# The low part of a turned block, subtracted from the PSUM bank itself instead of from an ACT copy

## The reference

```
h      = layernorm(x)                        # 2048 tokens x 256
gates, experts = top2(h @ router)            # two of eight experts for each token
y[t]   = sum over the two: gate * (act(h[t] @ W1[e] + b1[e]) @ W2[e] + b2[e])
x      = x + tanh(g) * (y + shared experts)
```

## Time and profile before

| | |
|---|---|
| median of 3 runs | 1986.92 us (1980.81 to 1989.0) |
| span of the profiled execution | 2007.2 us |
| PE busy | 1773.6 us (88%) |
| DVE busy | 1262.0 us (63%) |
| ACT busy | 975.4 us (49%) |
| POOL busy | 528.7 us (26%) |

### The profile page before, as it was taken

How to read it: one execution, slowest core, us unless ns; L and a number is a source line. 1 busy time by engine, 2 the same in 40 slices (tenths; PEclk the granted TensorE clock), 3 DMA queues, 4 the chain that set the end, 5 groups by cost and what they waited for, 6 DMA issues and landing times. The chain is left out here.

```text
span 2007.2 us, 32563 instructions
## 1 busy us (share of the span) xinstructions
PE 1773.6 (88%) x11808; PEld 1447.6 (72%) x11808; DVE 1262.0 (63%) x2310; ACT 975.4 (49%) x1739; POOL 528.7 (26%) x492
## 2 busy tenths in 40 slices
PE   6998899967799996699999969998899789798895
PEld 4667799922577775699999558886577566688884
DVE  6886488546245553588887566765434688656643
ACT  4652476413687671377776234443433255317730
POOL 2220343254333341222220630002000144213333
PEclk9998799988799996699999979999699899899997
DMA  3003377420100000567775220000000100026742
GB/s 109 17 17 126 121 255 248 132 61 0 49 1 12 6 12 25 203 225 229 246 238 169 81 102 1 1 1 1 22 1 1 57 12 12 30 79 208 235 127 81
DMA packets 97139, 178.32 MB, mean 89 GB/s; under 512 B 25184, under 2 KB 61946, under 8 KB 95914
## 3 DMA queue, kind: packets, MB, share of 16 engines
q1 hardware_dynamic: 85496, 146.00, 22.0%
q0 software_dynamic: 11232, 30.69, 5.2%
q10 hardware_dynamic: 288, 0.00, 0.0%
HBM read 149.38 MB, written 27.26 MB: 88 GB/s over the span
## 5 line engine op out<-in xcount | busy, mean ns | idle before, releaser
L1667 POOL DMA_INDIRECT f_block_rows_home<-normed_x,f_token_of_sb x138 | 168.3, 1220 | 451.4 <-PE psum L1713 324.5
L1693 PE MATMUL psum<-f_block_h_sb,f_w1h_home 128*128 128x256 f32 x736 | 211.4, 287 | 30.2 <-issue 10.7
L1693 PE MATMUL psum<-f_block_l_sb,f_w1h_home 128*128 128x256 f32 x736 | 206.8, 281 | 0.0
L1693 PE MATMUL psum<-f_block_h_sb,f_w1l_home 128*128 128x256 f32 x736 | 206.7, 281 | 0.0
L2316 PE MATMUL psum<-a_xT_home,context_w 128*128 128x256 f32 x704 | 182.2, 405 | 13.6 <-PEq L122 9.7
L1703 PE MATMUL psum<-f_w2h_home,f_hidden_h_home 128*128 128x256 f32 x644 | 187.4, 291 | 2.0 <-DVE f_hidden_l_home L1887 1.0
L1703 PE MATMUL psum<-f_w2h_home,f_hidden_l_home 128*128 128x256 f32 x644 | 181.7, 282 | 0.0
L1703 PE MATMUL psum<-f_w2l_home,f_hidden_h_home 128*128 128x256 f32 x644 | 181.7, 282 | 0.0
L1693 PEld LDWEIGHTS psum<-f_block_h_sb,f_w1h_home 128*128 128x128 f32 x736 | 140.8, 191 | 38.5 <-issue 28.6
L2316 PEld LDWEIGHTS psum<-a_xT_home,context_w 128*128 128x128 f32 x704 | 132.6, 198 | 45.3 <-issue 20.0
L2481 ACT ACTIVATE a_probsT_sb<-psum 77x1024 f32<-77x1024 f32 (+1 forms) x128 | 130.7, 1021 | 69.0 <-PE psum L2368 66.5
(11 more groups left out here) (314 smaller groups left out, 3986.6 us busy)
## 6 DMA issues: line engine op xcount, KB each, us to landing
f_w_sb<-in_f_w SPq DMA_DIRECT2D x161, 512.0 KB
sorted_y<-f_result_sb SPq DMA_DIRECT2D x69, 256.0 KB
normed_x<-f_xn_all SPq DMA_DIRECT2D x24, 256.0 KB, 2.1
f_b_row_sb<-in_f_b SPq DMA_DIRECT2D x46, 128.0 KB
f_w_sb<-in_f_w SPq DMA_DIRECT2D x23, 256.0 KB
f_block_rows_home<-normed_x,f_token_of_sb POOLq DMA_INDIRECT x138
residual<-in_x SPq DMA_DIRECT2D x8, 256.0 KB, 6.2
context_w<-in_a_wk SPq DMA_DIRECT2D x2, 1024.0 KB, 5.0
```

The source lines that it names most:

```text
L1667: nc.gpsimd.indirect_dma_start(block_rows[b % 2][:, h, :], None, xs, bass.IndirectOffsetOnAxis(ap=column, axis=0)).then_inc(sems[f"rows_in ...
L1693: last = nc.tensor.matmul(hid_ps(q)[:, m, :], w, rhs, start=(j == 0), stop=(j == len(parts) - 1))
```

## The change

ACT's plain copy of the turned bank and its two buffers `block_T` are dropped. DVE's subtract reads the bank itself as its first operand, and `block_h` as before as its second. Since DVE is now the last to read the bank, the turn that writes into it next waits for `block_low` in place of `turned_out`, and so does the wait at the layer's end before the banks pass to other work.

```diff
--- before.py
+++ after.py
@@ -1509,7 +1509,6 @@
     home = lambda k: [env["homes"][name, f"{k}{q}"] for q in range(2)]
     hidden_h, hidden_l, block_rows = home("hidden_h"), home("hidden_l"), home("block_rows")
     w1h, w1l, w2h, w2l = home("w1h"), home("w1l"), home("w2h"), home("w2l")
-    block_T = [sb(f"block_T{s}", [P, DC, BLOCK]) for s in range(2)]
     block_h = [sb(f"block_h{s}", [P, DC, BLOCK], F32R) for s in range(2)]
     block_l = [sb(f"block_l{s}", [P, DC, BLOCK], F32R) for s in range(2)]
     hidden = [sb(f"hidden{s}", [P, HC, BLOCK]) for s in range(2)]
@@ -1707,7 +1706,7 @@
         def turn(b, i, s):
 
             pe.wait_ge(sems[f"rows_in{s % 2}"], uses(i, s) * ROWS_IN + ROWS_IN)
-            pe.wait_ge(sems["turned_out"], b + 1)
+            pe.wait_ge(sems["block_low"], b + 1)
             for c in range(DC):
                 for h in range(BT):
                     last = nc.tensor.transpose(turn_ps(s % 2)[:, c, h * P:(h + 1) * P],
@@ -1775,7 +1774,6 @@
         def take(b, s):
             act.wait_ge(sems["turned"], b + 1)
             act.wait_ge(sems["block_low"], b + 1)
-            nc.scalar.activation(block_T[s][:], turn_ps(s), ACT.Copy)
             nc.scalar.activation(block_h[s][:], turn_ps(s), ACT.Copy).then_inc(sems["turned_out"], 1)
 
         def round_hidden(v, q):
@@ -1888,7 +1886,8 @@
 
         def split_block(b, s):
             dve.wait_ge(sems["turned_out"], b + 1 + 2)
-            low(block_l[s], block_T[s], block_h[s], "block_low")
+            nc.vector.tensor_tensor(block_l[s][:], turn_ps(s), block_h[s][:].bitcast(F32), ALU.subtract).then_inc(
+                sems["block_low"], 1)
 
         def body(b, i, s, ahead):
             for u in range(per_expert):
@@ -1988,7 +1987,7 @@
     def banks_left(pe):
         pe.wait_ge(sems["hidden_out"], UNITS * OUT + HIDDEN0)
         pe.wait_ge(sems["result_out"], RESULTS + RESULT0)
-        pe.wait_ge(sems["turned_out"], BLOCKS + 2)
+        pe.wait_ge(sems["block_low"], BLOCKS + 2)
 
     t.update(operands_left=operands_left, banks_left=banks_left, stated=stated, rows_places=rows_places)
```

## The result

The changed kernel takes 1968.66 us (median of 4 runs, 1964.88 to 1970.62); the kernel before, run beside it, takes 1986.23 (4 runs). The forecast was -9.8.

A forecast was written before the change was run, and what follows sets the result against it. f1 is bound by TensorE, f3 by a latency chain through ACT's plain copy, f0 by DVE's order. 20 x 0.49 = 9.8 us in f3, all other terms 0, took 1986.92 to 1977.1 us; range 1970.6 to 1985.

The forecast's parts named there:

- The chain and its blocks: In f3 the plain copy lies on the latency chain; dropping it saves 0.49 us in 20 blocks, 9.8 us.
- The starts: The two turned blocks taken ahead of each routed loop gain nothing: 0.
- Who ends the step: In f3 ACT stays later than DVE by 0.35 us; idle before the subtract about 0.37, PE's gap about 0.16.
- f0 and f1: In these layers dropping the copy frees ACT in time nobody waits for: 0; f0's gap stays 0.30 us.
- The PSUM read: DVE's subtract reading PSUM, on the chain in f0 and f3, costs 0, by equal 800 ns rows.
- the three-operand row: Fused form with a PSUM source, 751 ns at 128x512: the subtract's far end above, 67 ns more, 2.7 us.
- The rival with a dearer read: The subtract in f0 and f3 costs 2.7 us more, so the gain is 7.1: 1979.8 us; chance 0.12.
- the slower one: The subtract's PSUM read stretches under TensorE's writes, up to 0.38 us each: +5.8 us, 1992.7; chance 0.06.
- The DMA engines as the next bound: Rival: f3 would need 276 GB/s; with 258 as ceiling the gain is only 3.0 us, 1983.9; chance 0.10.
- The waits: A turn waiting for the subtract two blocks before, instead of the rounded copy, queues nothing new: 0.
- ACT's busy time: Over the whole kernel it was to fall by about 69 x 0.60 = 41 us.
- Which side of half a per cent: Whole kernel: forecast's 0.72 split into 0.38 beyond the 9.9 us line and 0.34 short of it.

The follow-up runs named there:

- after again: The changed kernel, unchanged, rerun with twelve runs and a second profile beside the kernel before: 1973.47 us, ratio 0.9949.
- Block first: In f0 and f1 DVE subtracts the turned block before the hidden values: on the changed kernel 1960.97 us (0.9901), on the kernel before 1973.36 us (0.9963).
- the PSUM read alone: Against the kernel before, DVE reads PSUM with the new waits, but ACT still makes its plain copy, unread: 1979.19 us, ratio 0.9972.
- before again: The kernel before, unchanged, run again for a second profile: 1982.75 us, ratio 0.9987.
- copy twice: DVE reads PSUM as in the change, but ACT makes two unread plain copies ahead of the rounded one: 1991.78 us, 1.0055 against the kernel before.

## Why the prediction was right, point by point

**The chain and its blocks.** Said: 20 blocks of f3 times 0.49, 9.8 us. Measured: 9.03 us over 19 steps, 0.475 a block, 9.5 for 20; between the two products that enclose the 20 blocks of the earlier trace rows, 110.11 us became 100.59, again 9.5. At equal clock the whole kernel is 9.8 us faster (after again). The typical loop block fell from 5.62 to 5.13 as said, those written out from between 5.35 and 5.45 to between 4.87 and 4.96. In every one of the 19 steps the way from the turn to the first products is 0.49 shorter (2.55 to 2.69 before, 2.06 to 2.20 after); what makes the mean step 0.475 here and 0.51 between the two later profiles is the stretch of products, which varies by 0.1 in either kernel.

**The starts: nothing.** In f3 the way from the first turn to the first products is 4.57 us in all eleven profiles, with the copy and without it.

**Who ends the step.** Idle time before the subtract: said 0.37, measured 0.38. PE's gap: said 0.16, measured 0.18. ACT is still the later of the two, as said: DVE's product ends at 1830.48 + 0.69 = 1831.17, the rounded copy at 1831.51.

**f0 and f1: nothing.** f0's gap stayed at 0.30 and its 19 steps at 127.2; f1 stayed at 11.65. The experiment with these two layers alone gives 1.0002. "Block first" shows what f0 was waiting for: the order on DVE.

**The PSUM read: nothing.** Said 0 by the row with the same operation, against 67 ns by the three-operand row. The subtract, all 69 of them, min/median/max:

```profile
L1889 DVE TENSOR_TENSOR f_block_l_sb<-psum,f_block_h_sb x69: 672/684/692, 226.4 to 1902.0; 128x512 fp32r<-128x512 f32 x69
```

684 ns from PSUM, 684 from SBUF in the earlier trace rows, 692 at most. The rival with a dearer read and the slower one, a stretch under TensorE's writes, both fall.

**The DMA engines as the next bound: fell.** f3 carries 257 to 259 GB/s at 0.80 to 0.81 of their time. The 276 GB/s of the sum were too much: it scaled the busiest stretch of the earlier trace rows; the mean of 219 and 251, times the same 1.098, is 258. That f3 now sits just at the supposed ceiling proves nothing either way, but "block first" moved 287 in f0.

**The waits: free,** by the experiment with the PSUM read alone.

**Mis-sized: ACT's busy time.** Said 69 x 0.60 = 41 us less, measured 975.4 - 943.5 = 31.9. Busy time is counted once where instructions overlap, and the two copies overlapped by 0.11; 69 x 0.48 is 33. The prediction had used the same overlap to price the chain at 0.49 and not 0.60, and left it out here.

**Wrong in size: the spread of the runs.** The range ended at 1970.6, and the first four runs have their median at 1968.66, outside it; by the ratio, 0.9924 of 1986.92, the time is 1971.8, just inside. The larger comparison gives 1973.47, inside it too. That the first figure came so close to the edge is the granted clock of four runs and not the chain, which gives -10.0 us at equal clock. The spread of three runs of before (8 us) was taken for that of the kernel; 29 runs later span 1971.06 to 1992.64. And the profiled span's 20 us above the median were taken as an even excess, and a profile's span as longer than the timed runs; they were two standing stretches of one execution, and the ten later spans, 1960.2 to 1989.5, each lie 1.8 to 3.0 us below their own execution's time. Here it did no harm, since neither stretch lay in a routed loop.

**Which side of half a per cent** was left nearly even within the forecast, 0.38 to 0.34. The first ratio says 0.76%, the larger one 0.51%: the gain is on that line, as worked out.

## What to carry to other kernels

Price a removed instruction by the distance between starts along the chain that ends the loop, and only in the blocks where that chain ends it: 69 copies of 0.60 us were worth 20 times 0.48. Where an engine comes out of other work just before the step, look at its order first; swapping two DVE instructions gave as much in f0 (9.4 us over 19 steps, and nothing in f1) as removing ACT's copy gave in f3. For effects of half a per cent, compare the loops themselves in the traces, and the runs at equal time at the lower clock.

## What the runs showed of the hardware

**Most of the spread between runs is the granted clock.** Every run but the first four of before has its mean granted clock on record. The time at the lower of the two levels (0.50; the granted clock in the traces of all eleven profiles is either this or 1.00) follows as 2 x (1 - mean clock) x span. Over the 75 runs of the kernel before that ran beside the nine experiments it goes from 232 to 279 us while the time goes from 1971.06 (mean clock 0.941) to 1992.64 (0.930): 0.47 us more for each microsecond more at the lower level, correlation 0.96. An estimate from the two levels is 0.50, for a stretch in which TensorE does nothing but work, its speed taken to go with the level. Near the end of the first profile of before, eight products `psum<-f_w2s,f_hidden_sb` of 128x256 took 1.99 us at 1.00 (from 1952.31) and 3.78 at 0.50 (from 1965.75). The column "at equal clock" is the mean distance of a kernel's runs from that line. The same stretch of the attention part in two executions, before again and after again, which have the same code there (the granted clock is the last figure but two):

```profile
716.00:720.00 4.00, 2.75 (x23) 1.57 (x24) 2.19 (x6) 1.83 (x4) 1.66 (x1) 0.90 0.19 66
724.00:730.00 6.00, 6.00 (x35) 4.02 (x34) 4.15 (x8) 4.34 (x11) 2.53 (x2) 0.50 0.00 0
```

```profile
716.00:720.00 4.00, 2.75 (x26) 1.85 (x24) 1.55 (x4) 1.89 (x6) 2.35 (x1) 0.86 0.20 70
724.00:730.00 6.00, 5.98 (x54) 4.68 (x53) 4.56 (x9) 6.00 (x18) 2.55 (x2) 1.00 0.01 3
```

In both TensorE was idle for 1.25 of the 4 us from 716 to 720. In one it then stays at 0.50 through 724 to 730 and does 35 products, in the other it is back at 1.00 and does 54. Why one execution comes back sooner isn't shown by any row; the code of the two is the same there.

**ACT's successive copies of the turned bank overlap** by 0.11 us when neither waits: copies of 0.60 us start 0.48 to 0.49 apart (1847.61 and 1848.10 in before, 1840.18, 1840.67 and 1841.15 in "copy twice"), so their durations can't be added up.

**A page's total can hold a passing stall.** One execution in eleven had 24 us of it in two places. The profile puts ACT's longest waits there down to "remote" (7.5 us) and to `residual<-in_x`, the load of the input (18.1 us), and neither tells what happened. A gain counted from two spans alone would have come out four times too large.
